# A DLRM tower on one core: five open gather groups, four one-hot buffers, earlier first transposes, and the third layer's weights applied on VectorE

## What is computed

```python
e = jnp.stack([tbl_0[ids[:, 0]], ..., tbl_25[ids[:, 25]]], axis=1)
combined = jnp.concatenate([dense_output[:, None, :], embeddings], axis=1)
interactions = jnp.einsum('bfd,bgd->bfg', combined, combined)
interactions_flat = interactions[:, iu, ju]          # above the diagonal
z = jnp.concatenate([dense_output, interactions_flat], axis=1)
h = jnp.concatenate([z, r_dense_output], axis=1)
h = jnp.maximum(h @ W_top1 + b_top1, 0.0)            # 607 -> 512
h = jnp.maximum(h @ W_top2 + b_top2, 0.0)            # 512 -> 256
y = h @ W_top3                                       # 256 -> 1
```

## Time and profile before

| what | us |
|---|---|
| median of 3 runs | 386.54 |
| lowest and highest run | 383.05, 386.66 |
| profiled execution, its own time | 385.73 |
| span of the profile | 383.8 |
| TensorE matmul busy | 357.0 (93%) |
| TensorE weight load busy | 329.9 (86%) |
| VectorE busy | 248.8 (65%) |
| ScalarE busy | 144.7 (38%) |
| GpSimd busy | 259.9 (68%) |

### The profile page before, as it was taken

The page is one execution under the profiler, slowest core; times in us unless marked ns, Lnnn a source line. Parts: engine busy times, 40 slices in busy tenths (PEclk is TensorE's granted clock), DMA queues, the critical chain, the costliest instruction groups (busy, mean ns, idle before and its releaser), DMA issues.

```text
span 383.8 us, 9905 instructions
## 1 busy us (share of the span) xinstructions
PE 357.0 (93%) x4248; PEld 329.9 (86%) x4248; DVE 248.8 (65%) x340; ACT 144.7 (38%) x370; POOL 259.9 (68%) x280
## 2 busy tenths in 40 slices
PE   0878699959999999999999999999999999999997
PEld 0777589849998999989998999989998999989976
DVE  2889978597483956668483957668573957533141
ACT  2578223723323423333323423333323423334241
POOL 5617767777777777777767777777777777777200
PEclk9989799989999999999999999999999999999999
DMA  7998574323323423334323423333223423222100
GB/s 161 227 243 194 138 234 98 98 75 79 84 63 97 104 71 80 90 92 102 81 70 91 108 67 85 90 89 100 84 70 91 92 68 85 65 66 58 35 4 0
DMA packets 20132, 36.73 MB, mean 96 GB/s; under 512 B 6157, under 2 KB 9877, under 8 KB 20090
## 3 DMA queue, kind: packets, MB, share of 16 engines
q0 software_dynamic: 8704, 17.84, 19.0%
q1 hardware_dynamic: 5338, 9.08, 9.8%
q10 hardware_dynamic: 6048, 9.18, 9.0%
HBM read 36.07 MB, written 0.01 MB: 94 GB/s over the span
## 4 chain that ended last, share of the span: by engine, by line
PE 84%; DVE 6%; DMA 4%; ACT 2%; issue 2%; SPq 2%; DVEq 0%; ACTq 0%
PE psB L435 35%; PE psG L461 15%; PE psB L510 9%; PE psB L419 8%; PE psB L517 8%; DMA ZH<-tbl 4%; PE psB L504 3%; DVE one_hot L734 3%; PE psB L472 2%; PE psB L522 2%; PE psB L489 2%; DVE tab_lo L745 1%; PE psB L486 1%; SPq L373 1%; ACT psB L616 0%
## 5 line engine op out<-in xcount | busy, mean ns | idle before, releaser
L360 POOL DMA_INDIRECT E<-tbl,gidx x272 | 259.1, 952 | 96.8 <-issue 79.6
L734 DVE TENSOR_TENSOR one_hot<-oidx,psR 125x1024 fp32r<-125x1024 int32 (+1 forms) x152 | 177.2, 1190 | 45.4 <-PE psB L435 40.3
L435 PE MATMUL psB<-one_hot,tab_hi 125*128 125x256 f32 x592 | 107.7, 304 | 11.4 <-ACT tab_hi L605 10.2
L435 PE MATMUL psB<-one_hot,tab_lo 125*128 125x256 f32 x592 | 99.7, 291 | 7.3 <-DVE tab_lo L740 3.8
L435 PEld LDWEIGHTS psB<-one_hot,tab_hi 125*128 125x128 f32 x592 | 83.8, 197 | 17.9 <-issue 13.0
L435 PEld LDWEIGHTS psB<-one_hot,tab_lo 125*128 125x128 f32 x592 | 84.7, 198 | 8.9 <-DVE tab_lo L745 4.8
L637 ACT COPY ET<-psB 128x512 f32<-128x512 f32 (+3 forms) x80 | 44.6, 575 | 60.4 <-PE psB L419 60.4
L461 PE MATMUL psG<-ET 128*52 128x52 f32 x2048 | 62.2, 214 | 1.0 <-issue 0.7
L461 PEld LDWEIGHTS psG<-ET 128*52 128x52 f32 x2048 | 54.6, 128 | 9.6 <-issue 3.5
L666 ACT COPY S<-psG 116x208 f32<-116x208 f32 x64 | 21.3, 333 | 63.3 <-PE psG L461 61.0
L419 PE MATMUL psB<-ident,E 128*128 128x128 f32 x272 | 42.6, 280 | 0.3 <-DVE w1p_lo L758 0.3
(11 more groups left out here) (54 smaller groups left out, 210.9 us busy)
## 6 DMA issues: line engine op xcount, KB each, us to landing
oidx<-hot_idx ACTq DMA_DIRECT2D x28, 256.0 KB
E<-tbl,gidx POOLq DMA_INDIRECT x272
ET<-tbl SPq DMA_DIRECT2D x3, 448.0 KB
oidx<-hot_idx SPq DMA_DIRECT2D x4, 256.0 KB
dense<-dense_pairs SPq DMA_DIRECT2D x8, 128.0 KB
ZH<-tbl SPq DMA_DIRECT2D x2, 448.0 KB
S<-tbl SPq DMA_DIRECT2D x2, 448.0 KB
oidx<-hot_idx ACTq DMA_DIRECT2D x7, 128.0 KB
```

The costliest lines, as they stand in the source:

```text
L360: nc.gpsimd.indirect_dma_start(E[:, n % SLOTS, i, :], None, gathered[feature_and_tile(n, i)[0]], bass.IndirectOffsetOnAxis(ap=gidx[:, 4 * ...
L435: product = nc.tensor.matmul(bank[:, t % 2 * DUO:(t % 2 + 1) * DUO], tab[0:ROWS_P, TABLE_BASE[t] + k0 + i, :], one_hot[0:ROWS_P, m % RING, ...
L734: nc.vector.tensor_tensor(one_hot[0:ROWS_P, m % RING, 0:many], ids, rows, ALU.is_equal).then_inc(hot_full[m % RING], 1)
```

## The change

It has four parts.

1. `E` gets five slots: GpSimd may have five groups open.
2. The one-hot ring shrinks from six buffers to four. The step at which VectorE waits stays where it was (chunk c used), but what is built there is the matrix of chunk c + 4.
3. In half 0 the turns are spread among all chunks but the first two, where it was all but the first five.
4. The third layer of duos 0 to 6: VectorE multiplies the two blocks of the second layer's output `h2` by their column of `w3s` and adds them, in two instructions behind its emptying of part 5. TensorE then sums over the partitions with one matmul by a column of ones, where it had two by columns of `w3s`. Duo 7 keeps the two.

```diff
-    SLOTS = 3
+    SLOTS = 5
-    RING = 6
+    RING = 4
...
         if h == 0:
-            return hots[:5] + spread(turns, hots[5:])
+            return hots[:2] + spread(turns, hots[2:])
...
+                elif d < DUOS - 1:
+                    pe.wait_ge(weighted, M2 * (d + 1))
+                    layer = nc.tensor.matmul(bank[0:1, 0:DUO], ones[:, :], h2[:, M2 - 1, :], start=True, stop=True)
                 else:
...
+            def weigh_outputs(d):
+
+                for q in range(M2):
+                    wait_out(dve, ("part", d, M1 + q))
+                    if q == 0:
+                        nc.vector.tensor_scalar(h2[:, 0, :], h2[:, 0, :], w3s[:, 0:1], None,
+                                                ALU.mult).then_inc(weighted, 1)
+                        continue
+                    dve.wait_ge(weighted, M2 * d + q)
+                    nc.vector.scalar_tensor_tensor(h2[:, q, :], h2[:, q, :], w3s[:, q:q + 1], h2[:, q - 1, :],
+                                                   ALU.mult, ALU.add).then_inc(weighted, 1)
...
                     elif step[0] == "part" and step[2] % 2 == 1:
                         empty_part(nc.vector, *step[1:])
+                        if step[2] == M1 + M2 - 1 and step[1] < DUOS - 1:
+                            if step[1] == 0:
+                                dve.wait_ge(weights_in, 16 * 4)
+                            weigh_outputs(step[1])
```

More of the change, by code:

```diff
@@ L247, in dlrm_program @@
         h2 = sb("h2", [P, M2, DUO], f32)
+        ones = sb("ones", [P, 1], f32)
         w2 = sb("w2", [P, M1, H2], f32)
@@ L295, in dlrm_program @@
         Zp_hi_ready = sem("Zp_hi_ready")
+        ones_ready, weighted = sem("ones_ready"), sem("weighted")
         bank_full, bank_out = sems("bank_full", BANKS), sems("bank_out", BANKS)
@@ L527, in _ @@
             pe.wait_ge(stacked_ready, 1)
+            pe.wait_ge(ones_ready, 1)
             for h in HALVES:
@@ L791, in split_pairs @@
                 split.then_inc(bank_out[PLACE["split", d, i][0]], 1)
+            def weigh_outputs(d):
[8 more added lines that the diff above has]
+                                                   ALU.mult, ALU.add).then_inc(weighted, 1)
             dve.wait_ge(ident_ready, 1)
+            nc.vector.memset(ones[:, :], 1.0).then_inc(ones_ready, 1)
             nc.vector.tensor_reduce(second[:, :], ident[:, :].rearrange("p (x s) -> p x s", s=PAIR)[:, :, 1],
```

## The result

The changed kernel takes 378.58 us in the median of 4 runs (377.52 to 379.89), the kernel before 384.8 in 4 runs (382.73 to 386.66). A repetition in a later series gave 0.9853 (0.9809 to 0.9898). The kernel before scatters more than its first three runs showed. In a later series its 35 runs lay between 382.59 and 388.04.

What follows compares the result with a forecast made beforehand. Behind 100 us TensorE's own order bounds the kernel; ahead of that, its waits for table remainders. Terms -2.9 - 0.1 + 0.6 - 2.1 + 1.0 - 0.4 = -3.9 us gave 382.6 us, range 379.5 to 386.0.

Steps and rivals of the forecast that it cites:

- the clock: TensorE behind the ninth table's wait: the low clock may or may not fall; -0.4 us, bounds 0 and -2.5.
- the clock stays up: Rival: the shortened ninth-table wait leaves TensorE's clock alone, weighing hidden; sum -6.6, so 379.9 us; chance 0.20.
- a start that moves by over 3 us: Sign at the kernel's start: a move by over 3 us either way makes the prediction wrong.
- The ninth table's wait: TensorE's start: the remainder stands behind three VectorE builds instead of five; -2.1 us, bounds -2.1 and -1.
- Earlier gathers delay the tables: Start, 18.5 to 27 us: gathers take DMA rate from the table queue; +1.0 us, bounds 0 and 1.7.
- Five groups are worth nothing to TensorE: GpSimd's long wait goes, but TensorE waits for no gather, so five open groups gain nothing directly; 0 us.
- The earlier turns: Start, half 0: TensorE's same work moves into a stretch where it waits anyway; cost 0, at most 0.2 us.
- The third layer: Part 6, one matmul instead of two: -2.9 us over duos 0 to 5, +0.6 for waits on weighing.
- duo 6: Last duo with the new third layer: gain lost because later transposes need VectorE's last gram copy; -0.1 us.
- that sum: Alternative for part 6 from the skill page: weighing pair just in time, wait term 0, sum 0.6 us lower.
- The ring of four later: From chunk 17 on, all 133 pairs of build and chunk are in time with four buffers; cost 0.
- The base: The sum was put on the median 386.54 us, not on the profiled execution of 385.73.

Runs made afterwards that it cites:

- experiment 2: The kernel before, six buffers kept, with the ninth table's remainder computed two builds earlier in VectorE's order: 383.13 us against 384.95, ratio 0.9952.
- experiment 7: The changed kernel with the ninth table's remainder two builds later and the bank clearing one build later: 384.55 us against 384.5 before, ratio 0.9978.
- experiment 1: The kernel before with only the one-hot ring cut from six buffers to four: 382.43 us against 384.95, ratio 0.9925.
- experiment 3: The kernel before with only the open groups raised from three to five: 386.34 us against 384.95, ratio 1.0031.
- experiment 12: The changed kernel with three open groups again instead of five: 379.93 us against 385.5 for the kernel before, ratio 0.9857.
- experiment 5: The kernel before with four one-hot buffers and five open groups, nothing else: 380.83 us against 384.5, ratio 0.9904.
- experiment 10: The changed kernel with the first weighing early and the ninth table's remainder one more build earlier: 376.29 us against 385.53 before, ratio 0.9759.
- experiment 4: The kernel before with only the third layer's weights applied on VectorE: 384.59 us against 384.95, ratio 0.9974.

## Why the prediction was wrong, point by point

**The step that failed: the clock.** It was bounded at 0 and -2.5 us and set at -0.4, "near the upper end, since a wait of over 2 us is left by the terms above". The wait left was 1.55 us, and the clock did not fall behind it. From chunk 15 to 19 the gain is 4.4 us, of which 2.3 are the wait and 2.1 are the work behind it at full clock. Experiments 2 and 7 show it from both sides, with the change's other parts absent in the one and present in the other. The granted clocks of all runs agree. This was the rival "the clock stays up", given 0.20 at 379.9 us. The sign that the prediction named for itself, a start that moves by over 3 us, has come true with these 4.4.

**The ninth table's wait.** -2.1 forecast, -2.28 measured. The mechanism is right: experiment 1 has it with the ring alone, experiment 2 with the place alone. I had not seen that the clearing of the gram banks must move with it, which the ring did (experiment 2: 1.80 us if not).

**Earlier gathers delay the tables.** +1.0 forecast and not seen. The two queues moved more together (2.21 against 2.09 MB), and their shares sum to 103.7% in either case, so a sum over 100% was no sign of engines that can't take more. Chunks 0 to 15 take 27.25 to 29.16 us in the eight profiles with five slots and 27.58 to 28.89 in the six with three, the means 28.0 and 28.3. The inference from two stretches of one profile took for a full engine what was the scatter of a run: this stretch makes up most of the 2.7 us between the spans of the two profiles of the changed kernel. Chunk 15 starts at 37.7 us in the mean of the eight and at 38.1 in that of the six, 0.4 us earlier with a 95% interval from 1.4 earlier to 0.6 later. So a delay of up to 0.6 us can't be excluded.

**Five groups are worth nothing to TensorE.** Half right. Alone they are worth nothing (experiment 3). But "it waits for no gather" was true of the kernel before, and TensorE 5 us earlier does wait, 2.3 us (experiment 1). The prediction had compared GpSimd and TensorE by their rates in a duo, and not by where GpSimd stands at the start. The earlier turns, priced at 0 on TensorE, would have done the same (experiment 12). The size of it in the times, 0.8 us between experiments 1 and 5 where the profiles have 2.7, stays open.

**A term that was missing: the first layer's weights.** TensorE's wait for the remainder of the dense weights fell. TensorE before, and after:

```profile
80.50 0.52 PE L472 MATMUL psB<-ident,S 116*128 116x116 f32 x3 [1.89 <-DVE w1d_lo L768]
```

```profile
73.35 0.52 PE L474 MATMUL psB<-ident,S 116*128 116x116 f32 x3 [1.35 <-DVE w1d_lo L774]
```

It is 1.34 or 1.35 us in all nine profiles with four buffers and 1.88 or 1.89 in the five with six. With four buffers the two builds in VectorE's order there are of chunks with three pieces, 0.94 us each, and before they had four, 1.21: 2 x 0.27 = 0.54 us.

**The third layer.** -2.9 for the matmuls, -0.1 for duo 6 and +0.6 for the waits, so -2.4. Measured from chunk 50 to 150, which holds six duos' third layers, 0.7 to 1.3 us in the five profiles with the weighing as in the change. A part saves 0.44 us instead of 0.48. The wait, 0.2 to 0.3 us a duo in the mean and not 0.1, is the term that was mis-sized: the second weighing takes 0.49 us where the row of a two-input instruction gave 0.42, and 0.47 us pass from the first one's start to the second's (115.03 to 115.50). The Trainium skill ("VectorE: DVE Perf Modes", "Mode 2x_2P") led to an estimate of 0.29 us for the first and to a wait of 0. Measured are 0.35 us in the profile after (single ones in the others took up to 0.56) and a wait, so the measurement decides against that sum. Duo 6 was right: its transposes wait for VectorE.

**The ring of four later.** Right. No profile with four buffers has TensorE waiting for a one-hot matrix in the steady duos. Behind chunk 19 the closest pair in the changed kernel is chunk 27, as worked out, with 1.8 us to spare. At the start it is closer than the working had it: chunks 18 and 19 found their matrices done only 0.5 and 1.0 us before, and in experiment 10 TensorE waits 0.16 us.

**The base.** The three runs known then had a median of 386.54, and the fourth brought it to 384.8. That moved the absolute time by 1.7 us. Against the base of four runs my -3.9 us would have been 380.9, and the range, moved by the same 1.7 us, would have held the result. The sum is 2.1 us short in either case, about as much as the clock's work behind the wait.

With the measured sizes the sum is -2.3 - 2.1 - 0.5 - 1.0 = -5.9 us, against 6.0 measured. That they meet within 0.1 is luck, since the 6.0 have an interval from 4.4 to 7.5 and the terms come from single profiles. The rival's sum of -6.6 was near by luck too: its third layer was 2.0 us too good and its tables 1.0 us too slow.

## What to carry to other kernels

A long wait of TensorE can cost more than itself: look at the granted clock behind it, and price a shorter wait with and without the slow stretch, as two cases, not with a value near one end. When an edit lets one engine run ahead, look for the next one behind it at its new position in time, not by the rates of the steady part. A pair of small instructions between a result and its consumer can be split, so that the part that needs only the earlier input lies in idle time.

## What the runs showed of the hardware

The clock of TensorE at the ninth table went with the length of one wait. In eight profiles with a wait of 1.55 to 1.57 us, and in one with 0.70, PEclk was 1.00 in all windows from 40 to 50 us. In five profiles with 3.81 to 3.83 us it fell to 0.50, the 1.2 GHz level. No run has a wait between 1.57 and 3.81 us there. The cost of the fall was not fixed: the low level lasted 3.4 us in one of the five, 6.8 in two and 10.2 in two. From chunk 15 to 34 the five needed 38.8, 38.2, 38.8, 40.3 and 40.3 us, the changed kernel 34.4.

Elsewhere shorter waits came before a low clock. In the profile of before, TensorE and its window earlier in the start:

```profile
23.28 0.74 PE L435 MATMUL psB<-one_hot,tab_lo 125*128 125x256 f32 x4 [1.66 <-DVE tab_lo L745]
```

```profile
26.00:28.00 2.00, 2.00 (x12) 2.00 (x10) 2.00 (x3) 1.35 (x2) 0.95 (x1) 0.50 1.03 233
```

The same happened in experiment 4 behind a wait of 1.13 us, and did not in experiment 2 behind one of 1.66 at 23.27. So the length of one wait alone doesn't decide it everywhere. A second pair of waits, of 1.35 or 1.88 us and of 2.08 us with half a microsecond of work between, went with a low clock in every profile, as here after:

```profile
76.00:78.00 2.00, 1.90 (x9) 1.68 (x10) 1.94 (x5) 1.30 (x5) 1.51 (x2) 0.58 0.63 173
```

A multiply of 128x256 fp32 by a column, from SBUF to SBUF on VectorE, took 0.348 us in the mean of the profile after, and a multiply by a column with an added second tensor 0.492. Over all profiles single ones took 0.34 to 0.56 and 0.48 to 0.55.
